# Self-attention of a Perceiver layer: value weight and output weight joined ahead of time, or applied one after the other

## What is computed

```python
q, k, v = y @ w_qkv            # 16 heads of 64
attn = softmax(q @ k.T / 8)    # 64 x 64 in each head and batch
out = attn @ v                 # 64 x 64 in each head and batch
x = x + concat(out) @ w_out    # 1024 -> 128
```

## Time and profile before

| | us |
|---|---|
| median of 3 runs | 2387.43 (2385.6 to 2388.24) |
| the profiled execution | 2386.94 |
| its span, first to last instruction | 2385.2 |
| TensorE busy | 2318.7 (97%) |
| VectorE busy | 2112.5 (89%) |
| GpSimd busy | 1491.8 (63%) |
| ScalarE busy | 1383.1 (58%) |
| mean granted TensorE clock | 0.997 of full |

### The profile page before, as it was taken

The page is one execution under the profiler, slowest core; times in us unless marked ns, Lnnn a source line. Parts: engine busy times, 40 slices in busy tenths (PEclk is TensorE's granted clock), DMA queues, the critical chain, the costliest instruction groups (busy, mean ns, idle before and its releaser), DMA issues. The chain is left out here.

```text
span 2385.2 us, 57754 instructions
## 1 busy us (share of the span) xinstructions
PE 2318.7 (97%) x16519; PEld 1971.5 (83%) x16519; DVE 2112.5 (89%) x3382; ACT 1383.1 (58%) x2594; POOL 1491.8 (63%) x1069
## 2 busy tenths in 40 slices
PE   7999999999999999999999999999999998999988
PEld 4667888888888888888888888888888888878756
DVE  8789999999999999999999999999999998568777
ACT  5844555555555555555555555555555554455646
POOL 3556777777777777777777777777777773001100
PEclk9999999999999999999999999999999999999999
DMA  3531222222222222222222222222222223531000
GB/s 97 192 95 46 55 54 54 54 54 54 54 54 54 54 54 54 54 54 54 54 54 54 54 54 54 54 54 54 54 54 54 54 48 107 166 107 38 2 2 18
DMA packets 442653, 145.07 MB, mean 61 GB/s; under 512 B 365360, under 2 KB 425680, under 8 KB 442448
## 3 DMA queue, kind: packets, MB, share of 16 engines
q1 hardware_dynamic: 442432, 143.50, 24.2%
q10 hardware_dynamic: 144, 0.52, 0.1%
HBM read 109.17 MB, written 34.73 MB: 60 GB/s over the span
## 5 line engine op out<-in xcount | busy, mean ns | idle before, releaser
L471 POOL TENSOR_TENSOR probs<-arena,best_all 128x1024 f32 (+2 forms) x397 | 943.6, 2377 | 427.7 <-DVE best L848 405.8
L1113 PEld LDWEIGHTS u_ps<-rows,probs 128*128 128x128 f32 x6656 | 802.7, 191 | 49.1 <-ACT probs L676 8.8
L1113 PE MATMUL u_ps<-rows,probs 128*128 (+1 forms) x6656 | 809.5, 275 | 7.9 <-ACT probs L676 4.9
L676 ACT ACTIVATE probs<-probs 128x1024 f32<-128x1024 f32 (+1 forms) x416 | 440.8, 1061 | 474.3 <-POOL probs L471 461.2
L833 DVE SCALAR_TENSOR_TENSOR arena<-s_ps,mask,rrms 128x512 f32 (+2 forms) x832 | 610.9, 735 | 95.7 <-PE s_ps L978 93.0
L634 ACT ACTIVATE squares<-k_ps 128x512 f32<-128x512 f32 (+1 forms) x832 | 474.7, 594 | 142.1 <-PE k_ps L978 118.5
L808 DVE TENSOR_REDUCE ssq<-squares 128x16 f32<-128x1024 f32 (+2 forms) x416 | 491.0, 1180 | 37.5 <-ACT squares L634 35.1
L848 DVE TENSOR_TENSOR best<-best,arena 128x1024 f32<-128x1024 f32 (+1 forms) x352 | 449.0, 1276 | 0.4 <-issue 0.2
L976 PE MATMUL k_ps<-w_hi,cT_hi 128*128 128x512 f32 (+1 forms) x832 | 363.7, 437 | 0.4 <-ACT squares L634 0.4
L976 PE MATMUL s_ps<-q_hi,cT_hi 128*128 (+2 forms) x832 | 330.2, 397 | 9.0 <-DVE arena L833 7.8
L978 PE MATMUL s_ps<-q_hi,cT_lo 128*128 (+2 forms) x832 | 328.9, 395 | 0.0
(11 more groups left out here) (257 smaller groups left out, 2236.7 us busy)
## 6 DMA issues: line engine op xcount, KB each, us to landing
stage<-in_ctx SPq DMA_DIRECT2D x1536, 16.0 KB, 1.7
rows<-in_ctx SPq DMA_DIRECT2D x32, 768.0 KB
queries<-probs SPq DMA_DIRECT2D x16, 1024.0 KB, 4.1
q_plain<-queries SPq DMA_DIRECT2D x32, 512.0 KB, 3.3
best_all<-best_rows SPq DMA_DIRECT2D x31, 512.0 KB, 3.8
u_transposed<-uT_sb SPq DMA_DIRECT2D x124, 128.0 KB, 2.6
a_uT<-u_transposed SPq DMA_DIRECT2D x10, 1024.0 KB, 4.9
arena<-u_transposed SPq DMA_DIRECT2D x6, 1024.0 KB, 4.9
```

The lines of the kernel that those rows point to most:

```text
L471: pool.tensor_tensor(probs[0:r, slot_of(c, PRING), :], scores_at(b, c), best_all[0:r, bass.ds((b % 2) * HL, HL)], ALU.subtract).then_inc(s ...
L676: act.activation(tile, tile, ACT.Exp).then_inc(probs_ready.sem, 1)
L1113: last = pe.matmul(u_ps[g // 3][:, at:at + UW], probs[0:r, s, g * P:(g + 1) * P], rows, start=(c == 0 and g % 3 == 0), stop=(c == NC - 1), ...
```

## The change

Self-attention's value weight stays as it is. `project_v` makes 1024 value columns (even heads, then odd ones) with 6 passes in place of 12, always in `tp`. `mix` takes the values as the stationary operand and yields, for each batch `b`, the turned heads in `ov[b]`. ScalarE evicts both banks to `oT`, behind Exp of the same step. `project_o`, between `project_v` and `score` on TensorE, multiplies `oT` by the output weight in eight fp32 products that add up in `ov[0]`. VectorE's one add to the residual waits for that. The joined weight, its transposes, product and evictions in the first part fall away, and of the four splits two stay, in steps -6 and -5. The output weight is loaded to another place of the arena, behind one more wait. The diff, cut to its core:

```diff
-    return {"wqkv": at(0, 3), "wv": at(3, 1), "wo": at(4, 1), "wout": at(5, 1), "wvo": at(6, 2), "wvo2": at(8, 2),
-            "wvT": at(10, 1), "wv2T": at(11, 1), "x": at(12, 1)[:, 0:X_EARLY * D], "qk": [at(10, 8), at(18, 8)], "v2": [at(0, 2), at(2, 2)],
+    return {"wqkv": at(0, 3), "wv": at(3, 1), "wo": at(4, 1), "wout": at(8, 1), "wvo": at(6, 2),
+            "wvT": at(10, 1), "x": at(12, 1)[:, 0:X_EARLY * D], "qk": [at(10, 8), at(18, 8)], "v": [at(0, 1), at(1, 1)],
...
+                    sp.wait_ge(shifted.sem, shifted.ended((B - 2) * NC + 8))
...
-            def save_wvo2():
-                for k in range(2):
-                    for odd in range(2):
-                        act.wait_ge(wvo_ps, 4 + 2 * k + odd + 1)
-                        at = odd * HL + k * HALF
-                        act.activation(w_now["wvo2"][:, at:at + HALF], (k_ps, s_ps)[k][odd][:, :],
-                                       ACT.Copy).then_inc(wvo2_saved, 1)
...
-                for banks, w in ((k_ps, w_now["wv"]), (s_ps, w_now["wqkv"][:, 2 * HL:3 * HL])):
-                    for g in range(PAIRS):
-                        last = pe.transpose(banks[g // 4][:, (g % 4) * P:(g % 4 + 1) * P], w[:, g * P:(g + 1) * P], ident[:, :])
+                for h in range(2):
+                    for g in range(4 * h, 4 * h + 4):
+                        last = pe.transpose(k_ps[h][:, (g % 4) * P:(g % 4 + 1) * P], w_now["wv"][:, g * P:(g + 1) * P], ident[:, :])
                     last.then_inc(post_turned, 1)
...
-            multiply_weights("wv2T", "wout", wvo_saved)
...
+                    for b in range(2):
+                        act.wait_ge(mixed, 2 * t + b + 1)
+                        act.activation(oT[:, :].rearrange("p (g b q) -> p b g q", b=2, q=L)[:, b],
+                                       ov[b][:, :].rearrange("p (g q) -> p g q", q=L), ACT.Copy).then_inc(oT_saved, 1)
...
-                if -6 <= i < -2:
-                    part = half(i + 6)
-                    act.activation(wvo2_hi[:, part], w["wvo2"][:, part], ACT.Copy).then_inc(wvo2_hi_ready, 1)
+                if -6 <= i < -4:
+                    act.activation(by_pair(wv_hi[:, half(i + 6)]), wv_of(i + 6), ACT.Copy).then_inc(wv_hi_ready, 1)
...
-                    for k in range(4):
-                        act.wait_ge(v_ps, 4 * t + k + 1)
-                        act.activation(w["v2"][t % 2][:, half(k)], four[k][:, :], ACT.Copy).then_inc(v_saved, 1)
+                    for k in range(2):
+                        act.wait_ge(v_ps, 2 * t + k + 1)
+                        act.activation(w["v"][t % 2][:, half(k)], tp[k][:, :], ACT.Copy).then_inc(v_saved, 1)
...
-                    dve.wait_ge(mixed, 2 * t + 2)
+                    dve.wait_ge(o_projected, t + 1)
                     link(dve.tensor_tensor(x2[:, cols(t)], ov[0][:, 0:D], x1[:, cols(t)], ALU.add))
-                    link(dve.tensor_tensor(x2[:, cols(t)], ov[1][:, 0:D], x2[:, cols(t)], ALU.add))
                     dve.sem_inc(x2_ready, 1)
                     spread_of(t, x2[:, cols(t)], z_stat, z_var)
                 if 0 <= i < 3:
...
-                            last = pe.matmul(ov[r][b * L:(b + 1) * L, 0:D], w["pT"][rows, at:at + L],
-                                             w["v2"][t % 2][rows, odd * HL + g * D:odd * HL + (g + 1) * D],
-                                             start=(g == 0), stop=(g == PAIRS - 1))
-                            if g == PAIRS - 1 and b == 1:
+                            last = pe.matmul(ov[b][odd * HD:(odd + 1) * HD, g * L:(g + 1) * L],
+                                             w["v"][t % 2][rows, odd * HALF + g * HD:odd * HALF + (g + 1) * HD],
+                                             w["pT"][rows, at:at + L], start=True, stop=True)
+                            if g == PAIRS - 1 and r == 1:
                                 last.then_inc(mixed, 1)
+
+            def project_o(t):
+                pe.wait_ge(oT_saved, 2 * t + 2)
+                for g in range(PAIRS):
+                    last = pe.matmul(ov[0][:, 0:D], oT[:, g * P:(g + 1) * P], w["wout"][:, g * D:(g + 1) * D],
+                                     start=(g == 0), stop=(g == PAIRS - 1))
+                last.then_inc(o_projected, 1)
...
                 pe.wait_ge(yT_lo_ready, 2 * t + 2)
-                pe.wait_ge(wvo2_ready, 4)
-                for k in range(4):
+                pe.wait_ge(wv_ready, 2)
+                for k in range(2):
                     pe.wait_ge(qk_saved, max(0, parts_upto(i) - 3 + k) if parts_upto(i) > parts_upto(i - 1) else parts_upto(i))
                     if k == 0:
-                        pe.wait_ge(v_saved, 4 * t)
+                        pe.wait_ge(v_saved, 2 * t)
                         pe.wait_ge(pT_saved, 2 * upto(i, 0))
-                        pe.wait_ge(added, upto(i, SUM_AHEAD))
-                        pe.wait_ge(yT_lo_ready, 2 * upto(i, TURN_Y_AHEAD))
-                    tokens = window(t, k // 2)
-                    pe.matmul(four[k][:, :], yT_hi[:, tokens], wvo2_hi[:, half(k)], start=True, stop=False)
-                    pe.matmul(four[k][:, :], yT_lo[:, tokens], wvo2_hi[:, half(k)], start=False, stop=False)
-                    pe.matmul(four[k][:, :], yT_hi[:, tokens], wvo2_lo[:, half(k)], start=False, stop=True).then_inc(v_ps, 1)
+                    tokens = window(t, k)
+                    pe.matmul(tp[k][:, :], yT_hi[:, tokens], wv_hi[:, half(k)], start=True, stop=False)
+                    pe.matmul(tp[k][:, :], yT_lo[:, tokens], wv_hi[:, half(k)], start=False, stop=False)
+                    pe.matmul(tp[k][:, :], yT_hi[:, tokens], wv_lo[:, half(k)], start=False, stop=True).then_inc(v_ps, 1)
...
...
                     project_qk(j, r, i)
                 if 0 <= i + V_AHEAD < TILES:
                     project_v(i + V_AHEAD, i)
+                if i >= 0:
+                    project_o(i)
                 if 0 <= i + S_AHEAD < TILES:
                     score(i + S_AHEAD)
```

More of the change, by code:

```diff
@@ L926, in step @@
                     turn_u(p - 2, c - LAG - 1)
-                if ending(p) and c < 4:
+                if ending(p) and c < 2:
                     save_turned_weights(c)
@@ L938, in save_turned_weights @@
             def save_turned_weights(k):
-                dve.wait_ge(post_turned, k // 2 + 1)
-                dve.tensor_copy(w_now[("wvT", "wv2T")[k // 2]][:, half(k % 2)],
-                                (*k_ps, *s_ps)[k][:, :]).then_inc(post_saved, 1)
+                dve.wait_ge(post_turned, k + 1)
+                dve.tensor_copy(w_now["wvT"][:, half(k)], k_ps[k][:, :]).then_inc(post_saved, 1)
             def save_wvo():
@@ L1120, in turn_weights, with multiply_weights @@
                 pe.wait_ge(last_columns, 2)
-                for banks, w in ((k_ps, w_now["wv"]), (s_ps, w_now["wqkv"][:, 2 * HL:3 * HL])):
-                    for g in range(PAIRS):
-                        last = pe.transpose(banks[g // 4][:, (g % 4) * P:(g % 4 + 1) * P], w[:, g * P:(g + 1) * P], ident[:, :])
+                for h in range(2):
+                    for g in range(4 * h, 4 * h + 4):
+                        last = pe.transpose(k_ps[h][:, (g % 4) * P:(g % 4 + 1) * P], w_now["wv"][:, g * P:(g + 1) * P], ident[:, :])
                     last.then_inc(post_turned, 1)
-            def multiply_weights(turned, w, saved):
+            def multiply_weights():
                 for k, banks in enumerate((k_ps, s_ps)):
@@ L1129, in multiply_weights @@
                         for odd in range(2):
-                            if j == 0:
-                                pe.wait_ge(saved, 2 * k + odd + 1)
                             rows = slice(odd * HD, (odd + 1) * HD)
                             g = slice((4 * k + j) * D, (4 * k + j + 1) * D)
-                            last = pe.matmul(banks[odd][:, j * D:(j + 1) * D], w_now[turned][rows, g], w_now[w][rows, g],
+                            last = pe.matmul(banks[odd][:, j * D:(j + 1) * D], w_now["wvT"][rows, g], w_now["wo"][rows, g],
                                              start=True, stop=True)
@@ L1495, in step @@
                     dve.tensor_tensor(wqk_lo[:, part], w["wqkv"][:, part], wqk_hi[:, part], ALU.subtract).then_inc(w_ready, 1)
[L1496 to L1500 removed]
+                if -6 <= i < -4:
+                    dve.wait_ge(wv_hi_ready, i + 7)
+                    dve.tensor_tensor(by_pair(wv_lo[:, half(i + 6)]), wv_of(i + 6), by_pair(wv_hi[:, half(i + 6)]),
+                                      ALU.subtract).then_inc(wv_ready, 1)
                 t = i
                 if t >= 0:
[L1503 removed]
+                    dve.wait_ge(o_projected, t + 1)
                     link(dve.tensor_tensor(x2[:, cols(t)], ov[0][:, 0:D], x1[:, cols(t)], ALU.add))
[L1505 removed]
                     dve.sem_inc(x2_ready, 1)
```

36 lines of the change are left out of this document (18 added, 18 removed).

## The result

The changed kernel takes 2406.63 us (median of six runs, 2404.46 to 2412.39), the kernel before 2387.69 us in the same comparison: ratio 1.0085, 95% interval 1.0075 to 1.0096. It is slower by 18.9 us. The forecast was 2399.5 with a range up to 2406.0, so the direction was right, and the measured time lies 7 us above the forecast and just outside the range. The profiled execution after took 2404.46 us, with a span of 2402.7 us. One run of the kernel before, out of the 27 beside experiments 5 to 7, took 6588.6 us and is left out of their ratios.

A forecast was written before the change was run, and what follows sets the result against it. Bound: a circle across VectorE, ScalarE and TensorE closing once a step. Losses of 19.2 us less gains of 6.8 gave +12.4, so 2399.3 profiled and 2399.5 us forecast, with a range of 2390.5 to 2406.

The forecast's parts named there:

- What bounds the kernel: Self-attention: a circle through VectorE, ScalarE and TensorE that closes once a step matters, beside each engine's sum.
- Prices on TensorE: Per step: values save 1.37 us, mixing 0.82, output products cost 1.88; net 0.31 saved in steps 0 to 13.
- Gains ahead of step 0: Before self-attention's step 0: dropped transposes, joined product, evictions, split and passes save 6.8 us.
- the eight transposes: Ahead of step 0: dropping the raw value weight's transposes from TensorE's unbroken run saves all 0.87 us.
- Steps from 0 on: Self-attention: a wait replaces work; steps 0 to 3 lose 5.1 us, 4 to 6 1.6, 7 to 10 3.9.
- Step 15's end: Behind step 15's mixing: evictions and output products, less savings in mixing and an add, cost 2.0 us.
- I leave it out, since the gaps have work close on both sides: Clock falls at TensorE's idle waits in steps 1 to 3 and 14, up to 6.8 us, were priced at nothing.
- the signs that the prediction named for being wrong: Self-attention: VectorE without its new wait, first six steps below 13.6 us, or a granted clock below 1.00.
- The clock falls: Rival: TensorE's clock falls at waits in step 14, perhaps also 1 to 3; 2401 to 2406 us, chance 0.16.
- Only the late steps lose: Rival: unseen slack lets steps 0 to 6 follow TensorE's sum and gain; 2390.6 us, chance 0.13.
- TensorE stays the bound: Rival: other work covers eviction and add throughout self-attention, so the kernel is faster; 2379.5 us, chance 0.08.
- The new mixing does what it says: Rival denied this: mixing might keep its old record rate, costing 0.8 us in steps 14 and 15 only.

The follow-up runs named there:

- experiments 5 to 7: Changed kernel with both reorderings, 2386.46 us; plus 12 transposes computing nothing in step 6, 2386.57 us; plus VectorE evicting the last step's second bank, 2386.07 us.
- experiment 4: Changed kernel without the output products and the evictions of mixed heads, part of the computation missing: 2363.68 us.
- experiment 8: Changed kernel with transposes that compute nothing in TensorE's waits of steps 1 to 3, 6 and 11 to 15: 2399.31 us.
- experiment 9: The changed kernel as it is, measured and profiled a second time: 2408.07 us.
- experiment 3: Changed kernel with ScalarE evicting the mixed heads ahead of the next Exp from step 6 on: 2397.15 us.
- experiment 6: Changed kernel with both reorderings and 12 transposes that compute nothing in TensorE's wait of step 6: 2386.57 us.
- experiments 1 and 8: Changed kernel with transposes computing nothing in TensorE's waits of steps 1 to 3 and 11 to 15, 2400.12 us; with step 6 too, 2399.31 us.
- experiment 5: Changed kernel with both reorderings, quantising ahead of VectorE's wait and eviction ahead of the next Exp: 2386.46 us.

## Why the prediction was wrong in size, point by point

- **What bounds the kernel** held: one circle a step, not TensorE's busy share. In the changed kernel TensorE is busy for 14.84 of 17.0 us in step 1 and for 8.64 of 12.5 in step 14, and its share on the page did not move.
- **Prices on TensorE** held. The eight output products last 1.95 us with a start-to-start of 1.88 (predicted 1.88), the new mixing 1.16 us (1.16, as the score), and what is narrower frees 2.2 us (2.19) in step 0 by experiment 4.
- **Gains ahead of step 0**: step 0 starts 9.3 us earlier, not 6.8. Of that 2.6 us are there at 83 us into the kernel, in a part that the change does not touch (ScalarE's first operation on `q_plain` starts at 80.5 instead of 83.1 us), and over the other profiles of this study, all of kernels with the change in them, that start lies anywhere from 79.8 to 82.2; there is one profile of the kernel before, so that whether the change or chance moved it stays open. Of the remaining 6.7 us, 4.2 lie in steps -10 to -1 (forecast 3.76) and 2.1 at the end of the first part (2.14). For the eight transposes (0.87) that leaves 0.4; behind those that remain TensorE now waits 0.49 us for an eviction of `u_sb`: I had taken all of their time as saved, and at most half of it was.
- **Steps from 0 on**: 13.3 (13.4), then at full clock 15.5 (15.5), 14.0 and 12.1 (14.1 and 12.2), 11.2 (11.1), 9.2 (9.15), 11.0 (11.2); by experiment 8 they sum to 183.0 us (183.5). Step 15's end was +1.9 (+2.0).
- **The step that failed** is "I leave it out, since the gaps have work close on both sides": it put the fall of the clock at nothing. A granted clock below 1.00 in self-attention was one of the signs that the prediction named for being wrong. The clock did fall: five times in the first profile, 7.1 us, at waits of 2.16 us (steps 1 to 3), 1.92 us (step 11) and 3.5 us (step 14) that all have dense work on both sides. A fall costs 1.3 to 1.6 us there, a little under the 1.7 us worked out from the earlier trace rows. The price was nearly right and the condition wrong. The profiled execution is 5.2 us above the 2399.3 that the sum gave for it: 7.1 us of falls and 0.8 us in the FFN, less 2.5 us by which step 0 starts earlier than forecast and 0.2 us in the other steps. The median is another 2.2 us above; experiment 9 shows a longer execution with more falls. TensorE's busy time by microsecond shows one of the falls, in step 1 of the changed kernel:

```profile
2135.00:2136.00 1.00, 0.00 (x0) 1.00 0.29 115
2136.00:2137.00 1.00, 0.36 (x1) 0.80 0.00 0
2137.00:2138.00 1.00, 1.00 (x3) 0.50 0.00 0
```

The clock is at 2.4 GHz until the wait is over and at half of it when TensorE is fully busy again: the fall hits the work behind the gap, and that work is on the chain. The Trainium skill, "TensorE: Matmul & The Clock Gate", section "HAM oscillation — how this bites in real kernels", tells of waits between bursts of matmuls that put the array back to half rate at each turn of a loop; the waits of its example are 3 to 5 us long. This trace agrees in steps 1 to 3, and with waits shorter than those, 2.16 us; in experiment 3 the same wait in step 1 was followed by no fall, so that it does not happen at each turn. The 2406.3 that the prediction worked out with four falls is the median within 0.3 us, and that is partly luck: the execution of 2404.46 us had five falls in steps 0 to 14, the one of 2413.03 us seven, and other terms were off by -2.5 and +0.8 us. I had held against it that self-attention shows clock 1.00 with small gaps; but the longest of those gaps in steps 0 to 14 is 1.2 us, so that row said nothing of gaps of 2.

- **The rivals.** "The clock falls" came true, with a chance of 0.16. "Only the late steps lose" falls with steps 1 to 3, and "TensorE stays the bound" with steps 1 to 14; once the eviction is moved (experiment 3), TensorE is busy for 9.63 of the 10.2 us of step 7, which comes close to that rival's condition by another edit. The new mixing does what it says.

**What stays open.** What decides at a wait of about 2 us whether the clock falls is not settled. In the first profile of the changed kernel 1.92 us in step 11 were followed by a fall, and 1.93 in step 13 and 2.01 in step 6 were not. In the kernel of experiment 4 TensorE waits 1.95, 2.15 and 2.10 us before the last query/key product of steps 1 to 3 and 2.01 in step 6, and steps 0 to 10 all show 1.00. Over the ten profiles of the changed kernel and its variants, TensorE has 27 waits of 1.9 to 2.2 us in steps 1 to 14; 16 of them were followed by a fall within 1.5 us of the end of the wait, and 11 were not. All four waits of over 3 us were followed by one, and of those of 1.3 us or less none. The 0.8 us more in the FFN goes with a mean granted clock of 0.94 from its first peak on, against 0.96 before (the kernel before has falls of its own there); what moves these falls, and the 2.6 us at the start of the kernel, were not traced further.

## What to carry to other kernels

When a change puts a new wait of about 2 us into an engine that was busy throughout, price a fall of TensorE's clock at each such wait, 1.5 us here. It came at 16 of 27 of them, so 0.9 us a wait is this kernel's mean (an estimate from these numbers), and the range of the forecast has to hold all of them falling. Before giving up such a change, look at what stands in each queue behind the new wait and ahead of its producer: two reorderings (work that needs nothing moved ahead of the wait, the eviction on the chain moved ahead of the Exp) took back all of the 19 us. An equal busy share on the page is no sign that two kernels have the same bound.

## What the runs showed of the hardware that was not expected

- The granted clock fell from 2.4 to 1.2 GHz behind waits of 1.92 to 3.5 us between dense work, and once in steps 0 to 14 behind 1.60 us (experiment 6), and stayed up in other executions at waits of 2.01 us with the same instructions around them. Each fall made its step 0.8 to 1.6 us longer. None came in the steps of experiments 1 and 8 that had transposes of the unit matrix in their waits, such as these, which end 0.83 us before the work goes on (step 1 of experiment 8):

```profile
2134.99 1.47 PE L1185 MATMUL a_sc<-ident 128*128 128x128 f32 x12
2137.29 0.50 PE L1593 MATMUL a_work<-a_yT_hi,a_wqk_hi 128*128 128x512 f32 x1 [0.83 <-DVE a_yT_lo L1489]
```

- The falls go with the spread: the changed kernel's eleven runs lie within 2404.5 to 2413.0 us, and the two longest have the lowest mean granted clock, 0.990. The five of experiment 8, whose profile has no fall left in steps 0 to 14, lie within 2399.08 to 2400.0, at 0.995 and 0.996. Five runs are few, and those of experiment 5, whose profile has none there either, spread over 7.9 us.
